# First attention of a fused transformer kernel: row maxima over 512 unmasked keys taken from one half's scores and the clipped difference to the other half

## The reference, cut to what matters

```python
NUM_HEADS = 32; NUM_KV_HEADS = 8; HEAD_DIM = 16
q = apply_rope(q, 0); k = apply_rope(k, 0)
k = jnp.repeat(k, GROUP, axis=1); v = jnp.repeat(v, GROUP, axis=1)
scores = jnp.einsum('bhqd,bhkd->bhqk', q, k) / math.sqrt(HEAD_DIM)
scores = jnp.where(causal[None, None, :, :], scores, jnp.float32(-1e+20))
attn = jax.nn.softmax(scores, axis=-1)
out = jnp.einsum('bhqk,bhkd->bhqd', attn, v)
```

## Time and profile before

| what | value |
|---|---|
| time, median of 3 executions | 1353.01 us (1350.63 to 1364.93) |
| profiled execution: its time | 1344.81 us |
| profiled execution: its span | 1343.1 us, mean granted PE clock 0.928 |
| PE, DVE, ACT, POOL busy | 1205.7, 953.5, 671.2, 375.2 us |
| chain that ended last | PE 64%, DVE 19%, issue 5%, POOL 5%, ACT 5% |

### The profile page before, as it was taken

The page is one execution under the profiler, slowest core; times in us unless marked ns, Lnnn a source line. Parts: engine busy times, 40 slices in busy tenths (PEclk is TensorE's granted clock), DMA queues, the critical chain, the costliest instruction groups (busy, mean ns, idle before and its releaser), DMA issues.

```text
span 1343.1 us, 21792 instructions
## 1 busy us (share of the span) xinstructions
PE 1205.7 (90%) x6800; PEld 753.2 (56%) x6800; DVE 953.5 (71%) x2990; ACT 671.2 (50%) x1023; POOL 375.2 (28%) x505
## 2 busy tenths in 40 slices
PE   4998999999899877998879999999988988879988
PEld 1875444443388865444868744444435887744368
DVE  5889889898166676653659798999962667576365
ACT  2621666666655452544436036666665554435542
POOL 0431411122254400114614323122213542002162
PEclk9996899999999997999979858999999999869999
DMA  8374411220010020100140742112200100120001
GB/s 317 120 196 87 125 29 26 57 65 3 1 49 1 1 47 19 55 2 0 63 175 23 189 130 70 26 26 57 66 2 0 50 1 17 32 72 2 1 8 56
DMA packets 37285, 76.20 MB, mean 57 GB/s; under 512 B 5084, under 2 KB 6620, under 8 KB 37036
## 3 DMA queue, kind: packets, MB, share of 16 engines
q1 hardware_dynamic: 37176, 74.82, 19.2%
HBM read 48.98 MB, written 27.08 MB: 57 GB/s over the span
## 4 chain that ended last, share of the span: by engine, by line
PE 64%; DVE 19%; issue 5%; POOL 5%; ACT 5%; DMA 1%; DVEq 0%; SPq 0%; ACTq 0%; POOLq 0%
PE bank L999 16%; PE bank L871 12%; PE bank L779 5%; PE bank L780 5%; PE bank L781 5%; DVE maxes L1208 5%; PE bank L983 4%; PE bank L977 3%; DVE unused L1204 3%; PE bank L765 3%; DVE ops L1152 3%; PE bank L881 2%; POOL x L1484 2%; POOL w_odd L1466 2%; ACT ops L1356 2%
## 5 line engine op out<-in xcount | busy, mean ns | idle before, releaser
L1431 ACT ACTIVATE probs<-bank 128x1024 f32<-128x1024 f32 (+3 forms) x416 | 367.9, 911 | 320.4 <-PE bank L983 220.3
L871 PE MATMUL bank<-ops 48*128 48x512 f32 (+3 forms) x960 | 321.8, 436 | 34.5 <-DVE maxes L1204 17.2
L1204 DVE CUSTOM_DVE_ANT_0 unused<-bank,causal 128x128 bf16<-128x128 f32 (+3 forms) x640 | 279.5, 486 | 47.7 <-PE bank L871 44.1
L1542 POOL TENSOR_SCALAR_AFFINE_SELECT probs<-probs 128x256 f32<-128x256 f32 (+1 forms) x256 | 118.8, 464 | 640.3 <-ACT probs L1431 640.0
L871 PEld LDWEIGHTS bank<-ops 48*128 48x128 f32 (+1 forms) x960 | 163.0, 206 | 218.9 <-DVE maxes L1204 96.0
L999 PE MATMUL bank<-probs,v_mem 128*17 128x512 f32 (+6 forms) x1920 | 252.2, 517 | 6.1 <-ACT heads_raw L1418 5.6
L1208 DVE TENSOR_REDUCE maxes<-bank 128x1 f32<-128x512 f32 x320 | 207.4, 684 | 40.7 <-PE bank L871 39.2
L983 PE MATMUL bank<-ops 50*128 50x512 f32 (+2 forms) x640 | 175.9, 448 | 5.0 <-ACT probs L1431 4.8
L779 PE MATMUL bank<-ops,xT 128*128 128x512 f32 (+1 forms) x288 | 116.2, 403 | 19.6 <-DVE x L1068 11.6
L983 PEld LDWEIGHTS bank<-ops 50*128 50x128 f32 x640 | 86.6, 197 | 57.9 <-ACT probs L1431 29.5
L1473 POOL TENSOR_TENSOR rstd<-var_eps,minus_half 128x1 f32<-128x1 f32 x96 | 52.7, 549 | 215.1 <-DVE var_eps L1046 214.5
(11 more groups left out here) (117 smaller groups left out, 1965.5 us busy)
## 6 DMA issues: line engine op xcount, KB each, us to landing
query_rows_dram<-ops SPq DMA_DIRECT2D x48, 256.0 KB, 3.8
ops<-query_rows_dram SPq DMA_DIRECT2D x64, 192.0 KB, 4.4
w_odd<-staging_wqkv SPq DMA_DIRECT2D x4, 1536.0 KB, 7.3
x<-x_dram SPq DMA_DIRECT2D x16, 256.0 KB, 6.1
ops<-ops SPq DMA_DIRECT2D x16, 256.0 KB, 3.0
out_dram<-x SPq DMA_DIRECT2D x16, 256.0 KB, 2.0
staging_wqkv<-wqkv_dram SPq DMA_DIRECT2D x2, 1536.0 KB, 15.8
key_rows_dram<-ops SPq DMA_DIRECT2D x24, 128.0 KB
```

Source lines behind the costliest of these rows:

```text
L871: last = mm(dst[:, h * w:(h + 1) * w], queries(a, u)[rows, t // 4, hi, t % 4 * P:(t % 4 + 1) * P], keys(a, u, hi)[rows, HALF * kp:HALF * k ...
L1204: V.tensor_tensor_reduce(unused[:, masked % 3, 0:w], part, causal[:, HALF - w:], 1.0, NEG, ALU.add, ALU.max, dst).then_inc(s["max_done"].s ...
L1431: A.activation(probs[:, e % 6, :, 0:cols], scores[:, 2 * (e % 2):2 * (e % 2) + 2, 0:cols], ACT.Exp, scale=a.scale).then_inc(s["exp"].sem, 1)
L1542: G.affine_select(out=p, in_=p, compare_op=ALU.is_ge, fill=0.0, base=0, pattern=pattern, channel_multiplier=-1).then_inc(s["masked"].sem, 1)
```

## The change: what it does

For a whole bank, PE no longer writes the scores of keys 0 to 511. Its moving operand is now two pieces of 256: keys 0 to 255, and the difference of keys 256 to 511 to keys 0 to 255 (`halved_keys`). The bank then holds a and b-a. ACT writes max(b-a, 0) to SBUF (`clip_difference`, a Relu over 256 columns, L1461 in the new file), and DVE takes the maximum of a + max(b-a, 0) over 256 columns with one `tensor_tensor_reduce` (L1255 in the new file). The bank is free again when DVE is done. The three places for clipped differences are memory of the mixture stage and `v_rest`, unused at that time.

Around it: DVE subtracts the two halves of the rotated keys once per sequence, after waiting for the rotation; the first key store writes 128 lanes instead of 64; two more loads bring the differences back; `xT` moves into the tensor `ops`, with no instruction more. The high and low split of these keys on ACT and POOL still covers 64 lanes (`rope_lanes`), so lanes 64 to 127 of what is stored as differences are what these regions held before. The amount of work of PE's matmuls, of ACT and of DVE doesn't depend on the values.

The order of banks changes too: within a query tile, two whole banks, half of the masked banks, two whole banks, the other half. On ACT, the clips of slot 0 stand between the two exponentials of a step, those of slots 1 and 2 behind the second.

```diff
+        if self.row_tiles == 2:
+            for t in range(4, NT):
+                at = [n for n, m in enumerate(self.max_banks) if m[0] == t]
+                first, second = ([self.max_banks[n] for n in at if self.max_banks[n][1] == kp] for kp in range(2))
+                half = len(second) // 2
+                self.max_banks[at[0]:at[-1] + 1] = first[:2] + second[:half] + first[2:] + second[half:]
...
+        def halved_keys(v):
+            first, second = 64 + 4 * v, 80 + v
+            return ops_flat.rearrange("p (n s) -> p n s", s=HALF // 2)[:, first:second + 1:second - first, :]
...
-            ops_of.tensor_tensor(prods[0:m, 1, :], prods[0:m, 1, :], prods[0:m, 2, :], ALU.add).then_inc(s["turned"].sem, 1)
+            last = ops_of.tensor_tensor(prods[0:m, 1, :], prods[0:m, 1, :], prods[0:m, 2, :], ALU.add)
+            if n == 0:
+                last.then_inc(s["summed"].sem, 1)
+                eng.wait_ge(s["summed"].sem, s["summed"].at(b, 1))
+                half = HALF // 2
+                last = ops_of.tensor_tensor(prods[64:P, 0:2, 0:half], prods[0:64, 0:2, half:], prods[0:64, 0:2, 0:half], ALU.subtract)
+            last.then_inc(s["turned"].sem, 1)
...
+            def load_key_differences(b):
+                sp.wait_ge(rope_stored[0].sem, rope_stored[0].at(b, 96))
+                for r in range(2):
...
+                    sp.dma_start(dst, k_rows[8:16].rearrange("(n r) p s -> r p n s", r=2)[r, :, :, 0:HALF // 2]
+                                 ).then_inc(key_differences_done.sem, 16)
...
-                    for h, (r, hi) in enumerate(heads_in):
+                    if n in a.halved:
+                        r, hi = heads_in[0]
+                        pe.wait_ge(key_differences_done.sem, key_differences_done.at(b, 32))
+                        rows = a.score_rows(r, a.part_rows)
+                        last = mm(dst.rearrange("p (n s) -> p n s", n=2), queries(a, u)[rows, 1, hi, t % 4 * P:(t % 4 + 1) * P],
+                                  halved_keys(u // 2)[rows], start=True, stop=True)
+                    for h, (r, hi) in enumerate(heads_in if n not in a.halved else ()):
...
+                        if a.paired[n] and paired >= 3:
+                            u3, k3 = divmod(paired - 3, len(a.paired_ops))
+                            dve.wait_ge(s["max_done"].sem, s["max_done"].at(b, u3 * a.unit_max_ops + a.paired_ops[k3] + 1))
...
+                        elif n in a.halved:
+                            k = a.over_at[i]
+                            dve.wait_ge(s["over"].sem, s["over"].at(b, k + 1))
+                            V.tensor_tensor_reduce(unused[:, paired % 3, 0:w // 2], src[:, 0:w // 2],
+                                                   over[k % 3].rearrange("p n c -> p (n c)"), 1.0, NEG,
+                                                   ALU.add, ALU.max, dst).then_inc(s["max_done"].sem, 1)
...
+            def clip_difference(b, st, i):
+                a, s = ATT[st], qs[st]
+                act.wait_ge(s["ring_full"].sem, s["ring_full"].at(b, i + 1))
+                A.activation(over[a.over_at[i] % 3].rearrange("p n c -> p (n c)"), ring[i % 3][:, HALF // 2:], ACT.Relu
+                             ).then_inc(s["over"].sem, 1)
...
+                            if n == 1:
+                                clip_differences(ring_no + len(a.ring_at[g][0]))
                             act.wait_ge(s["scored"].sem, s["scored"].at(b, e + 1))
...
+                    clip_differences(len(a.ring_first) + sum(len(slot) for step in a.ring_at[:g + 1] for slot in step))
```

More of the change, by code:

```diff
@@ L235, in plan_ring @@
         self.norm_at = [i for i, item in enumerate(self.ring) if item[0] == "norm"]
+        self.over_at = {i: n for n, i in enumerate(i for i, item in enumerate(self.ring)
+                                                   if item[0] == "max" and item[2] in self.halved)}
 A0 = Attention("rot", 32, 8, 16, 0.25, 2, True, ahead=1.07, slack=12)
@@ L357, in build @@
         inv_sum = sb("inv_sum", [P, 16])
+        over = [hw_mem[:, 0:2, :], hw_mem[:, 2:4, :], v_rest]
         work = probs.rearrange("p n c q -> p (n c q)")
@@ L496, in build @@
             s["max_done"] = signal(f"{n}_max_done", a.units * a.unit_max_ops)
+            s["over"] = signal(f"{n}_differences_clipped", a.units * len(a.halved))
             s["shift_step"] = signal(f"{n}_shift_step", 3 * a.units)
@@ L542, in build @@
         rope_lanes = [64, P, 64, P, P, P]
+        stored_lanes = [P, P, 64, P, P, P]
         @block.sync
@@ L612, in store_rope @@
                 _, hi, lo = rope_set(n % 2)
-                lanes, rows = (64, k_rows) if keys_only else (P, q_rows[16 * (n // 4):16 * (n // 4) + 16])
+                lanes = stored_lanes[n]
+                rows = k_rows[0:lanes // 8] if keys_only else q_rows[16 * (n // 4):16 * (n // 4) + 16]
                 rows = rows.rearrange("h (p m d) s -> p m h d s", p=3, m=2)
@@ L1193, in ring_read @@
                     t, kp, w, heads_in, diag = a.max_banks[n]
-                    masked = u * len(a.masked_ops) + sum(len(m[3]) for m in a.max_banks[:n] if m[4])
+                    paired = u * len(a.paired_ops) + sum(len(m[3]) for m, pair in zip(a.max_banks[:n], a.paired) if pair)
                     for h, head in enumerate(heads_in):
@@ L1408, in attention, with clip_differences @@
                 ns = len(a.steps)
+                ring_no = max(a.begun.values())
+                def clip_differences(upto):
+                    nonlocal ring_no
+                    for i in range(ring_no, upto):
+                        if i in a.over_at:
+                            clip_difference(b, st, i)
+                    ring_no = upto
+                clip_differences(len(a.ring_first))
                 for g in range(a.units * ns + a.lag + 2):
@@ L1594 @@
     rows = [nc.dram_tensor(f"{n}_dram", shape, F32, kind="Internal").ap()
-            for n, shape in (("key_rows", (8, 48, SEQ)), ("query_rows", (32, 48, SEQ)))]
+            for n, shape in (("key_rows", (16, 48, SEQ)), ("query_rows", (32, 48, SEQ)))]
     build(nc, w.pop("x"), w, scratch, *rows, out)
```

26 lines of the change are left out of this document (15 added, 11 removed).

## The result

The changed kernel takes **1433.94 us** (median of 4 executions, 1428.84 to 1443.22) against 1355.36 for the kernel before in the same session (1350.63 to 1364.93): a ratio of 1.058, interval 1.050 to 1.066. It is slower, and by more than the range of the prediction held. The profiled execution is the slowest of the four, 1443.22 us with a span of 1441.5; its mean clock (0.870) is near that of the others (0.873 to 0.876). The trace before is of a quick execution (span 1343.1), so the two traces lie 98.4 us apart where the medians lie 78.6 apart.

The account below looks back on a forecast made before the run. DVE, through the maximum strand, was taken to set the pace. 1344.8 + 32 (waits) - 2 (ahead of unit 0) + 1.5 (subtraction) = 1376.3; from the median, 1353.0 + 31.5 = 1385 us, 8-in-10 range 1320 to 1408.

Parts of the forecast that it names:

- The cost of clips and pairs: Whole banks in the first attention: an ACT clip takes 0.38 us, a DVE pair over 256 columns 0.42.
- the 4.1 forecast: DVE in a unit of the first attention: 16 whole banks, 0.26 us less each, save 4.1 us of work.
- The new wait: Whole banks go PE, ACT, DVE; clips wait behind exponentials, 0.47 us each, 7.6 in sum over the walk.
- bank A of step 4: First whole bank followed in the fourth step: clipped behind an exponential, DVE done at 2.29 us instead of 1.46.
- the term of 2.3 us a pass: Each of 14 first-attention passes gets 2.3 us longer, more than 6 lost in waits; taken as 32 us, bounds 18 to 53.
- the walk: One unit's region with whole banks, followed instruction by instruction: its end, the next join's start, moves from 18.66 to 21.0 us.
- PE's clock falls: Rival: more gaps bring PE the low clock in the units, 32 us on top, 1417 us; chance 0.05.
- The argument from the unit without maxima: Against the low-clock rival: there PE, busy 18.00 of 21.30 us, keeps clock 1.00.
- The clips fit into ACT's gaps: Rival: clips need 4.5 us of ACT's 6.8 idle in the region; 2.3 less a pass, 1321 us; chance 0.25.
- Its masked banks come in another order, at nothing by itself: PE in the first attention: the new order of masked banks costs nothing by itself.
- The prologue: Ahead of unit 0: -1 us a sequence, -2 in all, bounds 0 and -8; the subtraction separately +1.5.
- Unit 7 was to stay as it was: The unit with no maxima left to make should still take 21.3 us.

Follow-up runs that it names:

- t6_t7: Changed kernel in the old bank order, only the 8 whole banks of query tiles 6 and 7 halved and clipped, the others reduced as before; 1392.25 us.
- pause_long: As old_chain, plus one idle DVE reduce of 512 columns once a pass in the fourth step, result unused; 1394.19 us.
- load_only: As no_clip, but ACT runs as many Relus of the same size on an SBUF tile that nobody waits for; 1376.3 us.
- old_no_clip: Changed kernel in old bank order, banks halved, no clips, maximum over the first 256 keys alone; 1315.59 us in one run, 1320.47 in rounds.
- order_only: Changed kernel with no bank halved or clipped; new bank order and the work ahead of the attention stay; 1390.65 us.
- old_chain: Changed kernel with old bank order and no bank halved; subtraction, wider store, difference loads and operands' new place stay; 1354.39 us.
- pause_short: As pause_long, but the added idle DVE reduce reads 128 columns; 1352.81 us.
- old_clip: Changed kernel without the new bank order, ACT's first clip also waiting for the last QKV product; 1437.64 us.
- clip_first: Changed kernel with slot 0's clip ahead of the step's first exponential on ACT; 1454.27 us, 1.076 times the kernel before.
- no_clip: Changed kernel without clips: DVE's pair adds a constant tile, so the maximum covers the first 256 keys alone; 1322.34 us.

## Why the prediction was wrong

The direction and the first mechanism held, the size didn't: a second mechanism, PE's clock, was left out of the forecast and cost more than the first.

**What held.** The cost of clips and pairs came out within 0.01 us an instruction. DVE's busy time fell by about 3.2 us a pass (26.3 to 23.1), less than the 4.1 forecast. The new wait is the one described: bank A of step 4 lies behind an exponential, DVE behind it, PE behind DVE. Without the clock the term of 2.3 us a pass seems sized well, by two estimates, since no pass of the changed kernel is free of falls: the 8 clips of t6_t7 cost 1.0 at clock 1.00, twice that is 2; a line through the changed kernel's own passes (33.80 at 0.85, 35.49 at 0.76) reaches about 31 at 1.00, that is 2.7 above 28.26. With 2 to 2.7 a pass, 28 to 38 of the 82.7 us are waits, which matches the forecast's 32.

**What failed** is a step of the rivals: "in the walk PE never pauses as long as 1 us", on which the rival *PE's clock falls* got a chance of 0.05. The walk itself said otherwise: "scores to 1.14" and "bank B waits for A, 2.33" are 1.19 us without work. The trace has 0.94 to 1.11 there, in all 14 passes, and the clock falls behind it in 12 of 12, 0.1 to 3.5 us after its end. pause_long shows the rest: at this place 0.74 us once in a pass is enough. The other 45 to 55 us of the passes, what is left beside the waits, are put down to the clock, more than the rival's own 32, because its price was one fall of the trace before (2.3 us) and the falls here last longer: 3.2 to 3.9 us a pass.

The argument from the unit without maxima (PE busy 18.00 of 21.30 at clock 1.00, last of the earlier trace rows) reads the row rightly; that unit even has a pause of 0.75 us. But it is another mix of work, and what it bears did not carry over to a unit with maxima, where pause_long's 0.74 brings a fall every time. In the kernel before, no pass at full clock has a pause over 0.23 us, so no row could say what the walk's 1.19 would do there. The Trainium skill ("TensorE: Matmul & The Clock Gate", "A second HAM failure mode: psum-queue depth-cycling"), which I set aside by that row, says that short idle times between groups of matmuls can make the clock swing. By pause_long the trace agrees for the units with maxima; unit 7, with seven pauses of 0.33 to 0.75 us at clock 1.00, doesn't. As a rival it was priced too low (32 us) and given too small a chance.

**Other steps.** *The clips fit into ACT's gaps* is refuted by load_only and t6_t7: even clips that nobody waits for cost 0.9 us a pass at full clock, so the saving of 1.75 (old_no_clip) is half gone before the first wait. "Its masked banks come in another order, at nothing by itself" was nearly right at full clock (0.15 us) and wrong by the clock: 35 us between the passes of order_only and old_chain. This part of the sum had no range at all. The prologue was to give 2 us in all and cost 3.2 to the first join in the first sequence, with the subtraction (0.69 us as forecast, DVE L558) in it; 1.3 of the 3.2 are there before the change begins (DVE's first reads of products, 67.53 against 66.22). old_chain has 4.2 there without any clip, so it takes no hand-over ahead of unit 0 to lose as much. SP's added work was put at nothing, and no run separates it: the second key loads go out at 97.82 in old_chain and 99.21 in the changed kernel, against 94.82. Unit 7 was to stay as it was and grew by 2.0 and 5.3 us, with the clock low in it. The range added up from the prediction's own bounds is 1363 to 1409, not 1366 to 1408; that changes nothing.

**Open.** Why order_only falls in 9 of 12 passes is not settled: the trace shows no PE wait over 0.2 us near that point (208.06, 0.18 behind DVE), while pause_short with 0.34 five microseconds earlier falls once. The kernel before and old_chain fall 3 times in 12 at the same place, 16.3 to 16.7 us behind the join, with no wait over 0.15 us ahead of it; so part of the falls in the other kernels may come from whatever acts there. Why the clock of old_clip's pass from 202.96 outlasts a pause of 1.10 is open too. And of the 10.4 us behind the last join, 5.3 are in unit 7, and the rest was not traced.

## What to carry to other kernels

Before a change that adds a hand-over into a ring, follow the engine whose clock is granted, and write down each of its standstills and its place, beside the idle time in sum; neither the sum nor the longest one alone foretold the falls in all runs here. Price a clock fall by passes at either clock in the trace. Give it a large chance as soon as the walk shows a pause several times as long as any that the same stretch has now at full clock: here 1.1 us against 0.23. A cheap test is one idle instruction that makes the same pause, as in pause_long. Work moved to an engine that is idle a third of the time isn't free if its place in program order is behind long instructions: the 8 clips of t6_t7, 0.39 us each, made a pass at full clock 1.0 us longer, although they spared DVE 1.8 us of busy time. Releasing the bank earlier by moving the clip forward (clip_first) made it worse; a bank order that splits the pause was not tried.

## What the runs showed of the hardware

- A standstill of PE of 0.74 us, once in some 30 us in which it is otherwise busy, brought the low clock in 12 of 12 passes (pause_long); one of 0.34 us at the same place in 1 of 12 (pause_short). In another mix of work a standstill of 0.75 us left the clock at 1.00 (unit 7 of the kernel before), and one of 1.10 us was followed by 10 us at 1.00 in one pass of old_clip.
- The fall does not always follow at once: it comes 0.1 to 3.5 us behind the pause's end in the changed kernel, and 1.4 to 5.5 us behind it in pause_long. The low clock then lasts from 3.4 us (before) to 27.3 us (changed kernel, from 341.46), although PE is busy for nearly all of that time.
- The order of PE's banks alone, with the same instructions, moved the falls from 3 of 12 passes to 9 of 12 (old_chain, order_only).
- A microsecond at the low clock made a pass about 0.35 us longer in the kernel before (6.8 us low: 30.63 instead of 28.26).
- A matmul whose moving operand is two pieces of 256 columns cost nothing that shows beside one piece of 512: no_clip's passes, with 16 of them, are the shortest but for those of old_no_clip, which has them too.
